# The second experts' rows: scattered into tables and summed at the end, or added by the indirect DMA into the DRAM table of x2

## The reference

```
x  = x + 0.5 * ffn(layernorm(x))        # mixture of experts, first use
x2 = x + attention(layernorm(x))        # 16 heads, causal
out = x2 + 0.5 * ffn(layernorm(x2))     # the same mixture of experts, second use
```

## Time and profile before

| | |
|---|---|
| median of 3 runs | 1010.13 us (1009.66 to 1010.32) |
| the profiled execution, its device time | 1008.24 us |
| its span, first to last instruction | 1006.3 us |
| mean granted TensorE clock | 0.914 |
| PE busy | 818.1 us (81%) |
| DVE busy | 598.4 us (59%) |
| ACT busy | 522.7 us (52%) |
| POOL busy | 489.5 us (49%) |
| second mixture of experts, first row load to the end | 823.39 to 1006.3 us |

### The profile page before, as it was taken

One profiled execution on the slowest core, in us unless ns is written; L12 is line 12 of the kernel. 1 busy time (PEld: TensorE's weight loads), 2 busy tenths in 40 slices (PEclk: granted clock), 3 DMA queues, 4 the chain that ended last, 5 costly groups with the idle time before them and its releaser, 6 DMA issues. The chain is left out here.

```text
span 1006.3 us, 18072 instructions
## 1 busy us (share of the span) xinstructions
PE 818.1 (81%) x6599; PEld 444.1 (44%) x6599; DVE 598.4 (59%) x1237; ACT 522.7 (52%) x841; POOL 489.5 (49%) x686
## 2 busy tenths in 40 slices
PE   7469999963878888988879888888888509999990
PEld 7447877841323223332323323333133307787780
DVE  7941211223788878888877887868684423234335
ACT  6323243342347767678666786656677204334330
POOL 6047455415655552656468341662225642555453
PEclk9979999995669999999999999989799659999995
DMA  7215576531544161441623505242102125423236
GB/s 197 88 27 156 146 204 170 150 112 38 150 140 141 32 193 37 136 123 26 195 66 103 154 19 159 76 140 61 22 18 89 55 62 173 115 81 101 74 141 233
DMA packets 96184, 110.80 MB, mean 110 GB/s; under 512 B 12279, under 2 KB 68763, under 8 KB 96104
## 3 DMA queue, kind: packets, MB, share of 16 engines
q1 hardware_dynamic: 84968, 89.25, 29.9%
q0 software_dynamic: 9216, 17.98, 6.9%
q10 hardware_dynamic: 1920, 2.51, 0.7%
HBM read 57.86 MB, written 52.89 MB: 110 GB/s over the span
## 5 line engine op out<-in xcount | busy, mean ns | idle before, releaser
L1909 DVE TENSOR_REDUCE m_blk<-banks 128x8 f32<-128x1024 f32 (+1 forms) x320 | 349.5, 1113 | 62.8 <-PE banks L1507 51.0
L1830 ACT ACTIVATE pt<-banks 128x1024 f32<-128x1024 f32 (+3 forms) x384 | 300.7, 812 | 122.2 <-PE banks L1491 118.8
L1539 PE MATMUL banks<-pt,vs 128*32 128x512 f32 (+3 forms) x1536 | 170.8, 518 | 2.6 <-ACT o_sb L1770 2.4
L1491 PE MATMUL banks<-qb,kp 64*128 64x512 bf16 (+3 forms) x768 | 129.2, 342 | 44.2 <-DVE m_blk L1909 40.1
L2265 POOL TENSOR_SCALAR_AFFINE_SELECT pt<-pt 128x512 f32<-128x512 f32 x128 | 81.5, 637 | 167.3 <-ACT pt L1830 167.2
L1507 PE MATMUL banks<-kp,qa 64*128 64x128 bf16 (+4 forms) x1152 | 123.4, 288 | 20.0 <-ACT pt L1830 10.5
L845 POOL DMA_INDIRECT xe<-xn_rows,slot_tok x80 | 79.9, 999 | 91.4 <-PE banks L1186 34.4
L671 POOL DMA_INDIRECT y_tab<-ys,ids x70 | 68.0, 971 | 80.8 <-DVE ys L631 63.8
L1102 ACT ACTIVATE he<-banks,b_up 128x512 f32<-128x512 f32 (+1 forms) x96 | 57.9, 616 | 86.8 <-PE banks L1186 86.5
L1507 PEld LDWEIGHTS banks<-kp,qa 48*128 48x128 bf16 (+1 forms) x1152 | 45.0, 97 | 130.5 <-ACT pt L1830 94.7
L581 ACT ACTIVATE hT<-banks,bfc 128x512 f32<-128x512 f32 (+1 forms) x96 | 56.2, 615 | 84.6 <-DVE bfc L603 48.5
(11 more groups left out here) (339 smaller groups left out, 1127.4 us busy)
## 6 DMA issues: line engine op xcount, KB each, us to landing
bucket<-zero SPq DMA_DIRECT2D x16, 660.0 KB, 5.6
qb<-q_stack SPq DMA_DIRECT2D x32, 192.0 KB, 3.3
qa<-q_stack SPq DMA_DIRECT2D x30, 192.0 KB, 3.8
kp<-k_stack SPq DMA_DIRECT2D x30, 192.0 KB, 4.4
q_stack<-qp SPq DMA_DIRECT2D x18, 256.0 KB
k_stack<-kq SPq DMA_DIRECT2D x18, 256.0 KB
y_slots<-ye SPq DMA_DIRECT2D x16, 256.0 KB, 2.5
mid<-x SPq DMA_DIRECT2D x8, 512.0 KB, 3.4
```

Source lines behind the costliest of these rows:

```text
L1491: i = nc.tensor.matmul(ring[SLOT["score", 2 * u + pair]][:, s, 0:w], kp[g][rows_s, pair, kb * P:(kb + 1) * P], qb[par][rows_s, pair, q0:q0 ...
L1539: i = nc.tensor.matmul(o_bank[VW * h:VW * h + VW, q:q + w], vs[par][:, kb, h, :], pt[u % PTS][:, h, 0:w], start=u in (0, SECOND), stop=u i ...
L1830: nc.scalar.activation(pt[u % PTS][:, 2 * pair:2 * pair + 2, 0:w], ring[SLOT["score", 2 * u + pair]][:, :, 0:w], ACT.Exp, scale=SCALE).the ...
L1909: nc.vector.tensor_reduce(dst, ring[slot][:, :, 0:blocks * P].rearrange("p s (j k) -> p s j k", k=P), AX.X, ALU.max).then_inc(m_done, 1)
```

## The change

The tables `y_tab` and `y_last`, their zeroing, the loads of `mid`, `y_tab` and `y_last` at the end, the twelve adds on DVE and the SBUF tiles for them are gone. `mid` gets 1280 spare rows behind the 4096, zeroed by one store at the start of the attention block. Each of the eighty sends now names the row of `mid` by token number, or a spare row for an empty slot, and adds to it (`compute_op=ALU.add`). As a token may stand in two experts, all sends of an expert wait until all sends of the expert before have landed. At the end four DMAs, two from SP and two from ACT, copy `mid` to the output, from DRAM to DRAM.

```diff
-    mid = nc.dram_tensor("mid", [N, D], f32, kind="Internal").ap()
+    mid = nc.dram_tensor("mid", [N + CAP, D], f32, kind="Internal").ap()
-    y_tab = nc.dram_tensor("y_tab", [TOPK * N, D], f32, kind="Internal").ap()
-    y_last = nc.dram_tensor("y_last", [N, D], f32, kind="Internal").ap()
...
-                    for i in range(B):
-                        sp.dma_start(acc[i][:], by_rows(mid, 0, i)).then_inc(acc_ld, 16)
...
                     sp.wait_ge(sent[0], 16 * CT * (E // 2))
-                    sp.wait_ge(sent[1], 16 * CT * (E // 2 - 1))
-                    for i in range(B):
-                        for k in range(TOPK):
-                            sp.dma_start(tab[k][i][:], by_rows(y_tab, k * N, i)).then_inc(quarter_ld[i], 16)
-                    sp.wait_ge(sent_last, 16 * CT)
-                    for i in range(B):
-                        sp.wait_ge(sum_tab, i + 1)
-                        sp.dma_start(tab_l[i][:], by_rows(y_last, 0, i)).then_inc(quarter_ld[i], 16)
+                    sp.wait_ge(sent[1], 16 * CT * (E // 2))
+                    for i in range(0, B, 2):
+                        sp.dma_start(dest[i * S:(i + 1) * S, :], mid[i * S:(i + 1) * S, :]).then_inc(out_st, 16)
...
-                    for i in range(B):
-                        act.wait_ge(sum_all, i + 1)
-                        act.dma_start(by_rows(dest, 0, i), acc[i][:]).then_inc(out_st, 16)
+                    act.wait_ge(sent[0], 16 * CT * (E // 2))
+                    act.wait_ge(sent[1], 16 * CT * (E // 2))
+                    for i in range(1, B, 2):
+                        act.dma_start(dest[i * S:(i + 1) * S, :], mid[i * S:(i + 1) * S, :]).then_inc(out_st, 16)
...
-                        nc.vector.tensor_scalar(ti[:], xb[q][:, :, C_ID], SKIP - on, None, ALU.subtract)
+                        nc.vector.tensor_tensor(ti[:], xb[q][:, :, C_ID], spare_row[:], ALU.subtract)
...
-                        step(nc.vector.scalar_tensor_tensor(ti[:], one, -on, ti[:], ALU.mult, ALU.add))
                         step(nc.vector.tensor_tensor(ti[:], ti[:], used, ALU.mult))
...
-                        step(nc.vector.tensor_scalar(ids[q][:], ti[:], SKIP, None, ALU.add))
+                        step(nc.vector.tensor_tensor(ids[q][:], ti[:], spare_row[:], ALU.add))
...
-                    def send(e, q, table, rows_of, done):
+                    def send(e, q, before):
+                        wait_apart(pool, sent[1 - q], 16 * CT * before)
                         for cc, (t0, n) in enumerate(CHUNKS):
                             wait_apart(pool, y_ready, NC * e + cc + 1)
                             for t in range(t0, t0 + n):
                                 nc.gpsimd.indirect_dma_start(
-                                    table[:, :], bass.IndirectOffsetOnAxis(ap=ids[q][:, t:t + 1], axis=0), ys[q][:, t, :],
-                                    None, bounds_check=rows_of - 1, oob_is_err=False).then_inc(done, 16)
+                                    mid[:, :], bass.IndirectOffsetOnAxis(ap=ids[q][:, t:t + 1], axis=0), ys[q][:, t, :],
+                                    None, bounds_check=N + CAP - 1, oob_is_err=True,
+                                    compute_op=ALU.add).then_inc(sent[q], 16)
...
+                nc.vector.tensor_scalar(spare_row[:], iota_i[:, 0:CT], float(N), None, ALU.add)
...
-                    if g == 0:
-                        for table, row in ((y_tab, 0), (y_tab, N), (y_last, 0)):
-                            sp.dma_start(by_rows(table, row, b), zero[:, 0:T * D].rearrange("p (t d) -> p t d", d=D)
-                                         ).then_inc(tab_zero, 16)
...
                 sp.dma_start(x1[:], xf[0:S, :].rearrange("(t p) d -> p t d", p=P)).then_inc(x1_ld, 16)
+                sp.dma_start(mid[N:N + CAP, :].rearrange("(t p) d -> p t d", p=P),
+                             zero[:, 0:CT * D].rearrange("p (t d) -> p t d", d=D)).then_inc(tab_zero, 16)
```

More of the change, by code:

```diff
@@ L180, in macaron_block_kernel @@
         slot_of = sb("slot_of", [P, CT])
+        spare_row = sb("spare_row", [P, CT])
         sign = sb("sign", [P, T, TOPK])
@@ L426, in macaron_block_kernel @@
         NC = len(CHUNKS)
-        EXPERT_STEPS = 8
+        EXPERT_STEPS = 7
         def by_rows(table, at, piece):
@@ L456, in experts @@
             sent = [sem(f"sent{tag}{i}") for i in range(2)]
-            sent_last, acc_ld, sum_tab, sum_acc, sum_all, out_st = (
-                sem(f"{n}{tag}") for n in ("sent_last", "acc_ld", "sum_tab", "sum_acc", "sum_all", "out_st"))
+            out_st = sem(f"out_st{tag}")
             with ExitStack() as part:
@@ L472, in experts @@
                 ids = [sbe(f"ids{tag}{i}", [P, CT], i32) for i in range(2)]
-                acc = [sbe(f"acc{tag}{i}", [P, T, D]) for i in range(B)]
-                tab = [[sbe(f"tab{tag}{k}{i}", [P, T, D]) for i in range(B)] for k in range(TOPK)]
-                tab_l = [sbe(f"tab_l{tag}{i}", [P, T, D]) for i in range(B)]
                 block = part.enter_context(nc.Block())
@@ L598, in turned, with numbers @@
                                               t_bank[(g + NC * q) % 2][:, 0:n * P]).then_inc(t_evac, 1)
-                    def numbers(e, q, use, last=False):
+                    def numbers(e, q, use):
                         step = Steps(dve, e_chain, e * EXPERT_STEPS, EXPERT_STEPS)
@@ L608, in numbers @@
                         used = used.rearrange("p o t -> p (o t)")
-                        on = 0.0 if last else float(N)
-                        nc.vector.tensor_scalar(ti[:], xb[q][:, :, C_ID], SKIP - on, None, ALU.subtract)
+                        nc.vector.tensor_tensor(ti[:], xb[q][:, :, C_ID], spare_row[:], ALU.subtract)
                         step(nc.vector.tensor_tensor(pd[:], xb[q][:, :, C_P0], xb[q][:, :, C_P1], ALU.subtract))
@@ L634, in expert @@
                     def expert(e, q, use, more):
-                        numbers(e, q, use, not more)
+                        numbers(e, q, use)
                         dve.wait_ge(w_ld[q], 48 * use + 48)
@@ L671, in send @@
                                 nc.gpsimd.indirect_dma_start(
-                                    table[:, :], bass.IndirectOffsetOnAxis(ap=ids[q][:, t:t + 1], axis=0), ys[q][:, t, :],
-                                    None, bounds_check=rows_of - 1, oob_is_err=False).then_inc(done, 16)
[L675 to L681, removed]
+                                    mid[:, :], bass.IndirectOffsetOnAxis(ap=ids[q][:, t:t + 1], axis=0), ys[q][:, t, :],
+                                    None, bounds_check=N + CAP - 1, oob_is_err=True,
+                                    compute_op=ALU.add).then_inc(sent[q], 16)
+                    send(0, 0, 0)
+                    send(1, 1, 1)
+                    with nc.gpsimd.Fori(1, E // 2) as h:
+                        send(2 * h, 0, h)
+                        send(2 * h + 1, 1, h + 1)
                     pool.wait_ge(sent[0], 16 * CT * (E // 2))
-                    pool.wait_ge(sent[1], 16 * CT * (E // 2 - 1))
-                    pool.wait_ge(sent_last, 16 * CT)
+                    pool.wait_ge(sent[1], 16 * CT * (E // 2))
         U = NT // 2
@@ L1470, in _ @@
                 wait_apart(sp, x2_st, 16 * B)
-                sp.wait_ge(tab_zero, 16 * 3 * B)
+                sp.wait_ge(tab_zero, 16)
             @block.tensor
```

## The result

The changed kernel takes 1032.61 us (median of 4 runs, 1028.58 to 1035.0) against 1009.89 us for the kernel before (4 runs): ratio 1.0218, 95% interval 1.0174 to 1.0262. It is slower, by 1.7 to 2.6%, where 1005.7 us was forecast. Rival 1 of the prediction happened.

The account below looks back on a forecast made before the run. PE was taken to bound the kernel until 973.5 us, then a tail without PE. Last sends landing at 992.1, wake-up 0.05 and copy 9.7 gave 1001.9 against 1006.3; 1010.13 less 4.4 made 1005.7 us, range 1000.5 to 1036.

Parts of the forecast that it names:

- Rival 1: POOL becomes the bound, with p above 1.35 but below 1.75; 1027.6 us at p of 1.6; chance 0.26.
- p: Time of one adding send on POOL: taken as 1.15 us, between 0.97 (plain send) and 1.94 (plain send twice).
- d: Extra landing time of an adding send for reading the old row: between 0 and 1.15 us, taken as 0.5.
- 10p + 4.61 + d - 18.62: Lateness per expert: sends, landing and way to the next send, less PE's 18.62 us; zero at p of 1.35.
- The wait costs nothing with plain sends: POOL's wait before an expert's first send: 14.6 us from first send to last landing, hidden under 18.62 us.
- The copy, 9.7 us: At the end, 2 MB DRAM to DRAM replaces load, add and store: 9.7 us, between 7.85 and 13.2.
- rival 3: The copy at the end eats the gain, taking 13 to 15 us; 1010 us in all; chance 0.08.
- DVE's slow sends go: Last expert's sends beside DVE's long adds return from 1.96 and 1.97 to 0.97 us; 0.47 us beside weighting stays.
- Zeroing, spare rows, `numbers`: 0: Removed zeroing, added spare-row store and one DVE step fewer per expert: each hidden, 0 us; first two at most 1.
- 2 us is what a measurement can tell: Smallest difference in whole-kernel time taken as measurable: 0.2%, about 2 us.
- rival 4: DMA engines add row by row, waiting a landing each: 9.2 us a send, 590 us more; chance 0.05.
- Rival 2: An adding send takes twice a plain one on POOL, 1.94 us; 1054.8 us in all; chance 0.10.

Follow-up runs that it names:

- the plain kernel: The changed kernel with the add taken out of its sends, wait and copy kept; ratio 0.9894 to the kernel before, 154.0 us from first send to end.

## Why the prediction was wrong

The step that failed is "For p I take 1.15", with its reason that a constant 0.97 "looks like a fixed cost more than a cost per row". The observation was right: rows cause 1.0 ns each of a plain send, 0.12 of its 0.97 us. The conclusion wasn't, for a fixed cost can be another one for another operation, and it is: 1.25 for 0.85 us. The trace of the kernel before has no adding send and couldn't tell, and the bounds, 0.97 and 1.94, hold the 1.55. The decision between them rested on one argument that spoke only of rows.

The mechanism was on record with its threshold. For p = 1.55 and d = 0.5 the prediction's 10p + 4.61 + d - 18.62 makes 2.0 us late per expert; 2.83 were measured. The terms that were too small are the landing, 3.54 us on average from the send's start for the 3.2 of the sum (3.15 to 4.46), and the way to the next send, 1.15 for 0.76 (nine steps took 16.76 for 16.65). Over seven experts that is 0.84 x 7 = 5.9 us more. With p = 1.55 the prediction's own sum would have given 1023.6 us (2.0 x 7 late, then 16.65, 0.47, 3.2 and 9.75 behind 975.81), so the choice of p makes 17.9 of the 26.9 us that the forecast was off, and the landing and the way to the next send 5.9. The 3.1 left are less than the spread ahead of the first send.

Point by point otherwise:

- *The wait costs nothing with plain sends*: shown, ratio 1.003 (0.9994 to 1.0066).
- *d = 0.5*: right for five of the seven landings that POOL stood for, 3.2 - 1.55 - 1.15 = 0.5; the other two, 4.46 and 4.25, make 1.76 and 1.55, outside the bound of 1.15. Beside these two, SP's loads moved 0.47 and 0.37 MB on queue q1, beside the five nothing; that they cause it is not tested.
- *The copy, 9.7 us*: 9.0 measured, so rival 3 fell. The load alone took 7.85 and load, add and store 13.2, so reading and writing do overlap.
- *DVE's slow sends go*: yes; in the plain kernel nine steps take 11.76 us (975.08 to 986.84) for 14.19, the one beside the weighting included. In the changed kernel the last weighting falls beside sends of expert 6, so the 0.47 us that the sum kept for it is not there.
- *Zeroing, spare rows, `numbers`: 0*: no sign of a cost, but the time ahead of the first send spreads over 14.4 us, so one of 1 us would not show.
- *2 us is what a measurement can tell*: too little; in one set of 29 runs the kernel before took from 1002.35 to 1015.75 us.
- *The DMA engines follow*: yes, so rival 4 fell, though they do much more than the prediction allowed (below).
- *Rival 2, the reading that all of a send is descriptors*: fell, 1.55 measured for 1.94. By the Trainium skill (GPSIMD Engine Reference, When to use GPSIMD) one core writes the read descriptors of such a DMA and another the write descriptors, and (Collectives: The Full Stack, The bandwidth ceiling) the add of a collective's reduce step takes two read descriptors where a copy takes one. The part of a send that grows with the rows, 2.3 ns for 1.0, would agree with that; the 0.40 us that doesn't grow is extra, and what POOL does in it no run shows.

Put together: the gain that the sum expected was real, 6.8 us with plain sends; making them add cost 25.2.

## What to carry to other kernels

Before a DMA is made to do arithmetic, measure its issue on the engine that issues it: the 1.55 us of one such send in a profile would have shown that p lies above the prediction's own 1.35. Where a chain of sends is made to wait for itself, compare the steps between its sends, plus the landing of the last one, plus the way to the next send, with the pace of what feeds it. Here that was 16.76 + 3.54 + 1.15 = 21.45 us against 18.62. Below the pace the wait is free, above it every round pays. A cost that doesn't vary within one operation need not be the same in another operation.

## What the runs showed of the hardware

An adding send is cut differently in the DMA engines. Queue q0 while the sends run (packets, MB, share of 16 engines), in the changed kernel (845 to 1010 us, 74 sends), answers to the earlier trace rows:

```profile
q0 software_dynamic: 10369, 4.72, 30.9%
```

The plain sends of the kernel before left the rows of empty slots out. The changed kernel with plain sends moves all rows, as the adding one does (850 to 980 us, 70 sends):

```profile
q0 software_dynamic: 2234, 4.57, 9.9%
```

That is 140 packets an adding send where a plain one has 32, and 0.69 us of each engine (0.309 x 165 / 74) where a plain one took 0.18 (0.099 x 130 / 70). With 64 rows an adding send has 79 packets (6240 for 79 sends), so 61 packets go with 64 rows, about one a row. That is 3.7 times the work, and still hidden beneath the 1.85 us of a step.

A copy of 2 MB from DRAM to DRAM in four DMAs from two queues took 9.0 us, little more than the 7.85 us of loading as much alone.
